# Four chunks' degree comparisons moved from the second place's end to the third place's first tiles in a four-layer graph kernel

## The reference

```python
def _sage_conv(x, src, dst, Wl, Wr, b):
    agg = jax.ops.segment_sum(x[src], dst, num_segments=n)
    deg = jax.ops.segment_sum(jnp.ones_like(dst, dtype=x.dtype), dst, num_segments=n)
    mean = agg / jnp.maximum(deg, 1.0)[:, None]
    return mean @ Wl + x @ Wr + b
h = jnp.maximum(_layernorm(x, axis=-1), 0.0)
h = jax.nn.relu(_sage_conv(h, src, dst, Wl1, Wr1, b1))
h = jax.nn.relu(_sage_conv(h, src, dst, Wl2, Wr2, b2))
h = jax.nn.relu(_sage_conv(h, src, dst, Wl3, Wr3, b3))
return x + _sage_conv(h, src, dst, Wl4, Wr4, b4)
```

## Time and profile before

| what | value |
|---|---|
| median of 3 runs | 664.71 us (664.27 to 666.58) |
| profiled execution | 668.48 us, span 666.7 us |
| PE busy | 620.0 us, 93% of the span |
| DVE busy | 276.5 us, 41% |
| ACT busy | 181.2 us, 27% |
| mean granted TensorE clock | 0.977 of full speed |

### The profile page before, as it was taken

The page is one execution under the profiler, slowest core; times in us unless marked ns, Lnnn a source line. Parts: engine busy times, 40 slices in busy tenths (PEclk is TensorE's granted clock), DMA queues, the critical chain, the costliest instruction groups (busy, mean ns, idle before and its releaser), DMA issues.

```text
span 666.7 us, 9640 instructions
## 1 busy us (share of the span) xinstructions
PE 620.0 (93%) x3836; PEld 340.4 (51%) x3837; DVE 276.5 (41%) x524; ACT 181.2 (27%) x385; POOL 38.8 (6%) x87
## 2 busy tenths in 40 slices
PE   5567998959999998999999999999999999999998
PEld 4333555435555554544444445444445655646586
DVE  6785896667788877940211211211120100101011
ACT  3684866327364461320110100212110000000000
POOL 8000400000000000000000000000001011010110
PEclk9986999979999999999999999999999999999999
DMA  8301211321121211315342441334540123032131
GB/s 261 95 1 21 90 20 30 134 65 37 7 84 32 83 34 22 78 39 174 106 121 80 124 113 48 101 95 117 143 119 18 41 82 111 0 111 72 39 111 32
DMA packets 64990, 51.52 MB, mean 77 GB/s; under 512 B 36712, under 2 KB 49549, under 8 KB 64946
## 3 DMA queue, kind: packets, MB, share of 16 engines
q1 hardware_dynamic: 64590, 50.31, 26.3%
q0 software_dynamic: 240, 0.37, 0.2%
q10 hardware_dynamic: 116, 0.24, 0.1%
HBM read 28.71 MB, written 16.62 MB: 68 GB/s over the span
## 4 chain that ended last, share of the span: by engine, by line
PE 84%; DVE 5%; ACT 5%; issue 2%; POOL 1%; DMA 1%; SPq 1%; DVEq 0%; ACTq 0%; POOLq 0%
PE agg_ps L2313 33%; PE window_ps L2313 18%; PE lin_ps L2231 5%; PE window_ps L2151 5%; PE lin_ps L2248 5%; PE lin_ps L2207 4%; PE lin_ps L2108 3%; PE lin_ps L2256 2%; PE window_ps L2289 2%; PE agg_ps L2289 2%; ACT counts L1868 2%; PE turn_ps L2151 1%; DVE aggT L1624 1%; PE turn_ps L2027 1%; PE degree_ps L2337 1%
## 5 line engine op out<-in xcount | busy, mean ns | idle before, releaser
L2313 PE MATMUL agg_ps<-counts,H 128*128 128x512 f16 (+3 forms) x1026 | 235.2, 355 | 12.3 <-DVE aggT L1624 12.3
L2313 PEld LDWEIGHTS agg_ps<-counts,H 128*128 128x128 f16 (+1 forms) x1026 | 79.5, 99 | 68.9 <-issue 21.9
L1868 ACT ACTIVATE counts<-window_ps 128x400 f16<-128x400 f32 x150 | 73.2, 504 | 70.0 <-PE window_ps L2151 57.7
L1514 DVE TENSOR_TENSOR counts<-early 128x2048 f16<-128x2048 bf16 x66 | 78.7, 1217 | 15.6 <-PE window_ps L2151 12.8
L2313 PE MATMUL window_ps<-counts,early 128*128 128x512 f16 (+2 forms) x346 | 77.6, 379 | 0.0
L2313 PE MATMUL window_ps<-counts,H 128*128 128x512 f16 (+2 forms) x291 | 55.3, 346 | 0.0
L2313 PEld LDWEIGHTS window_ps<-counts,early 128*128 128x128 f16 (+1 forms) x346 | 33.7, 98 | 41.4 <-issue 3.4
L1624 DVE SCALAR_TENSOR_TENSOR aggT<-agg_ps,columns,rdeg 128x512 f32<-128x512 f32 (+1 forms) x27 | 16.9, 658 | 80.6 <-PE agg_ps L2313 77.1
L1174 POOL TENSOR_TENSOR newH<-newH,plan 128x256 f32<-128x256 f32 (+1 forms) x25 | 17.3, 724 | 553.6 <-DMA newH<-in_x_dram 553.6
L2151 PEld LDWEIGHTS window_ps<-counts 128*128 128x128 f16 x412 | 31.0, 99 | 33.5 <-issue 5.6
L1514 DVE TENSOR_TENSOR early<-early 128x1024 f16<-128x1024 bf16 (+1 forms) x69 | 43.9, 684 | 8.9 <-PE window_ps L2151 7.4
(11 more groups left out here) (234 smaller groups left out, 636.6 us busy)
## 6 DMA issues: line engine op xcount, KB each, us to landing
selfT<-hT_d SPq DMA_DIRECT2D x18, 512.0 KB, 4.3
rdeg<-rdeg_d SPq DMA_DIRECT2D x24, 256.0 KB, 4.1
hT_d<-newT SPq DMA_DIRECT2D x12, 512.0 KB, 4.5
counts<-in_x_dram SPq DMA_DIRECT2D x6, 512.0 KB, 8.1
hT_d<-counts SPq DMA_DIRECT2D x6, 512.0 KB, 3.1
newH<-in_x_dram SPq DMA_DIRECT2D x6, 512.0 KB
out_dram<-newT SPq DMA_DIRECT2D x5, 512.0 KB
hT_d<-newT SPq DMA_DIRECT2D x6, 256.0 KB, 3.9
```

Of the source, the lines that this page charges most:

```text
L1514: v.tensor_tensor(hots_of(group).rearrange("p r a (n d) -> p r a n d", d=2), pairs.unsqueeze(1).unsqueeze(1).broadcast_to([P, n, 2, P // 2 ...
L1868: a.activation(counts[:, :, 2 * w * WIN:2 * (w + 1) * WIN].rearrange("p t (a w) -> p a t w", a=2), window_bank(FILL_AT[w])[:, 0:2 * KEYS]. ...
L2313: last = m((agg_ps, window_ps)[bank][:, h, 0:n], tile[:, part, h * P:(h + 1) * P], counts[0:rows_, k, chunk_cols(c, n)], start=first and p ...
```

## The change

`cut_steps(3)` to `cut_steps(6)` are no longer called in the second place (at k = 16 and 21) but in the third place, before the steps of k = 0, 1, 2 and 3, one each. The sums of the cuts on TensorE stand at k = 3, 6, 9, 12 instead of 2, 6, 10, 14, the copies on ScalarE at k = 4, 7, 10, 13 instead of 3, 7, 11, 15, and the inversion on VectorE at k = 22 instead of 23.

```diff
-        LATE_SUM_K, LATE_TAKE_K, LATE_INVERT_K = (2, 6, 10, 14), (3, 7, 11, 15), 23
+        LATE_CUT_K, LATE_SUM_K, LATE_TAKE_K, LATE_INVERT_K = (0, 1, 2, 3), (3, 6, 9, 12), (4, 7, 10, 13), 22
...
-                            16: lambda: (cut_steps(3), cut_steps(4)), 20: lambda: copy_turned(1, 0, 0),
-                            21: lambda: (cut_steps(5), cut_steps(6))}
+                            20: lambda: copy_turned(1, 0, 0)}
...
                     if q >= 2 and k == ADD_K:
                         add_own(q - 1)
+                    if q == 2 and k in LATE_CUT_K:
+                        cut_steps(3 + LATE_CUT_K.index(k))
                     if q == 2 and k == LATE_INVERT_K:
                         invert_degrees(2)
```

## The result

The changed kernel takes 662.01 us (median of 11 runs) against 666.31 for the kernel before (11 runs, among them the three that the prediction started from): a ratio of 0.9938, 95% interval 0.9922 to 0.9954, so 4.3 us or 0.6% faster. The median of before is 1.6 us above that of those three runs alone, 664.71. The profiled execution of the changed kernel has a span of 659.6 us.

What follows compares the result with a forecast made beforehand. TensorE was taken to bound the kernel, stalled 7.32 us while VectorE's comparisons held 4.26 us of the path. 3.55 us (earlier restart) + 0.46 (clock) = 4.0, from 664.71 to 660.7 us; range 658.9 to 663.6.

Steps and rivals of the forecast that it cites:

- What bounds it: Between second and third place: TensorE idles 7.32 us for VectorE's aggT, with comparisons holding 4.26 us of that path.
- Part 1: Comparisons leave the second place: TensorE restarts at 138.76, 3.55 us earlier, with the register load and waits partly exposed.
- My bound of 4.26: Upper bound on the earlier restart, in us, if low_part covers the register load and waits entirely.
- Part 2: Comparisons in the third place, counted from TensorE's restart T: 1.1 us of waits for tables at full clock, none at low.
- Part 3: Clock behind TensorE's shortened pause of 3.8 us: 1.71 us lost in place of 2.17, a gain of 0.46 us.
- the milder form: Clock low for 3.42 us, as at the second place's start, all of it behind TensorE's restart in the third place.
- The clock stays up: Rival: no low clock behind the restart, but 1.1 us of waits for tables; gain 4.6, 660.1 us; chance 0.15.
- Part 4: Cuts' sums, copies and inversion at other tiles: counted as 0 us, with no wait of the inversion for the columns.
- Long low: Rival: the clock falls early and stays low 6.82 us, 5.94 behind the restart; gain 2.75, 662.0 us; chance 0.12.
- tables late in full: Rival: TensorE pays all 4.26 us in the third place at full clock; gain 1.5, 663.2 us; chance 0.13.
- slower: Rival: third-place waits for tables keep the clock low 13.6 us; change of -5.3, 670.0 us; chance 0.05.
- nothing at the restart: Rival: a wait the trace does not show ends TensorE's pause, so nothing changes; 664.7 us; chance 0.07.

Runs made afterwards that it cites:

- e1: Kernel before with only the new tiles for the cuts' sums, copies and inversion, comparisons left at the second place's end; ratio 1.0001 to before.
- e4: Kernel before with all eight comparisons at k = 14 of the second place, in VectorE's idle time ahead of low_part; ratio 0.9932 to before.
- e7: Changed kernel with VectorE's register load of four words moved to k = 5 of the second place, ahead of low_part; ratio 0.9947 to before.
- e9: Changed kernel unchanged, profiled a second time, one execution; 42.74 us from low_part's start to the third place's scaling.
- e6: Changed kernel with each of the eight comparisons made twice in the third place; ratio 1.0006 to before.
- e10: Changed kernel unchanged, profiled a third time, one execution; 42.31 us from low_part's start to the third place's scaling.
- e5: Changed kernel with the comparisons spread to k = 2, 5, 8, 10 of the third place instead of 0, 1, 2, 3; ratio 0.9916 to before.
- e8: Kernel before with comparisons at k = 14 and register load at k = 5 of the second place, and its scaling ahead of the next tables; ratio 0.9902 to before.
- e3: Changed kernel with 12 extra matmuls, their sum thrown away, filling TensorE's pause at the third place's start; ratio 0.9947 to before.

## Why the prediction was right

The forecast was 4.0 us with a median of 660.7. The measured difference is 4.3 us by the medians and 4.1 by the ratio; 662.01 lies in the range. It is 1.3 us above 660.7 because the median of before is 1.6 us higher over 11 runs than over the three. Two sizes of the sum were off in opposite directions, the restart by 0.47 us and the clock's term by some 0.15, so the nearness of 4.0 to 4.3 is in part luck.

- **What bounds it.** Right: the comparisons stood on the path, and without them TensorE restarted 4.02 us earlier. e1 shows that the rest of the change alone brings nothing, and e4 that the comparisons bring the gain without it.
- **Part 1, mis-sized.** I took the first table at 1.37 us behind `low_part`'s start (136.08); it came at 0.89, and e7 puts the load's share at 0.2. The 0.78 us that I read between the load's end and the second group's wait in the chain held the gap of 0.41 us, which no wait explains and which did not stand ahead of the first table in the changed kernel. So 3.55 should have been 4.02. By my own sign (a restart later than 139.6) part 1 stood; the idle of some 0.6 us behind `low_part` was 0.23. My bound of 4.26 held.
- **The Trainium skill's floor for a tensor_load,** about 600 ns (page "DMA: Bandwidth & Descriptors", section "Latency and other measured facts"), does not hold here: 0.375 us again in the changed kernel.
- **Part 2, right.** I had the third and fourth group ready at T + 3.5 and T + 6.6; they were at T + 3.49 (139.73 - 136.24) and T + 6.57. At full clock I expected waits of 0.5, 0.3 and 0.3 us for the third, fourth and fifth group; they are 0.60, 0.32 and none by their rows. The 1.1 us in all cost 1.25 (see e9), since a sum with its steps took 0.61 us ahead of the third group and not 0.66, so TensorE wanted it earlier. With a low clock I expected none, and e9 has none. The reckoning of groups against sums was worth its trouble: e6 shows that past it each microsecond on VectorE costs TensorE one.
- **Part 3, wrong where it names one case.** "I take the milder form, 3.42 us low" got a chance of 0.48, the clock up 0.15. The profile and e10 have it up, e9 down; e5 and e7, with nearly the same pause, have it up. By my own sign ("a low clock of 6 us or none") this part failed in the profile, whose course was that of the rival "The clock stays up". The time is hardly moved, since the waits for tables fill the place of the slow clock: 42.74 and 42.32. Before, the low clock cost 2.17 or 1.4 us; after, it costs nothing, or 0.4 net. For the two profiles the terms are 4.02 + 2.17 - 1.25 = 4.94 of the 5.00 us measured in the place.
- **Part 4, right.** The inversion has no wait. The moved copies do bring TensorE one more wait of 0.36 us for ScalarE, in e1 as well, whose length at full clock is 0.1 us shorter than before all the same.
- **The rivals.** Long low, tables late in full, slower, and nothing at the restart did not occur. e6 is what the slower one would have needed: it takes twice the comparisons to bring the kernel back to 1.0006, and even its waits of 1.63 and 2.88 us brought no low clock behind them.
- **A slip in the range.** 658.9 is 1.2 us below the clock-up rival's 660.1, not 1.4; nothing hangs on it.

The mean of the length is 46.8 us for the kernel before (47.32, 46.58 and e1's 46.45) and 42.5 for the change (42.32, 42.74, 42.31): 4.3, which is the measured difference. The restart gives 4.02 of it, and 0.3 are the clock's saving less the waits for tables, where my term was 0.46.

## What to carry to other kernels

Work that an engine did between the last operand and the hand-over that another engine waited for cost in full here (4.02 of 4.26 us came back); look first for the idle time of the same engine just ahead of it (here 4.81 us), then for room behind the hand-over. Behind it, count the ring, the three groups of tables that may exist at a time: work in small pieces between two groups brought no wait, the same work in two blocks did (e5 against the change, 1.25 us at equal work). And try the hand-over itself ahead of everything that the waiting engine needs only later (e8, where it was one of three edits).

## What the runs showed of the hardware

- The clock fell in e3 while TensorE was busy by its records in the whole stretch before, with the cuts' sums, 80 of 102 of at most 16 columns. The stretch with 110 matmuls, the fall behind it (at 159.56, by the mean of 0.78) and the last stretch of low clock (until 162.98, mean 0.51):

```profile
155.00:159.00 4.00, 4.00 (x110) 3.52 (x109) 1.77 (x3) 1.71 (x4) 0.00 (x0) 1.00 0.02 5
159.00:160.00 1.00, 1.00 (x15) 0.63 (x11) 0.00 (x0) 0.00 (x0) 0.00 (x0) 0.78 0.00 0
...
162.00:163.00 1.00, 1.00 (x7) 0.63 (x6) 0.01 (x1) 0.78 (x3) 0.00 (x0) 0.51 0.00 0
```

  It was low for 3.42 us and cost 1.7. In the other executions the same sums left the clock alone, so that the narrow sums cause the fall is not shown.
- One program's clock differs between executions: behind the pause of 3.3 us it stayed up in four profiles (the change twice, e5, e7) and fell in two (e6, e9). The four had a low clock at the second place's start too (from about 114 or 115 us, over 3 us long), the two had none there; no run tests whether the one hangs on the other. Single profiles of one kernel differ in length by 0.4 us (the change) and 0.7 us (before) with their clocks, and by 1.7 between e3 and the change.
- VectorE's sequencer had gaps of 0.41 us that no wait explains (e4 and before, above); the one before lay under the comparisons and cost nothing, the one of e4 made its restart 0.4 us later.
